# Issuing one third of the FFN weight reloads from GpSimd instead of SyncE in a macaron block

## The reference

```python
x = x + 0.5 * ffn(layernorm(x))
x = x + attn(layernorm(x))
x = x + 0.5 * ffn(layernorm(x))      # the same weights as the first

def ffn(x):                          # 2048 tokens a core
    shared = sum over 2 experts of (silu(x @ wg_s) * (x @ wu_s)) @ wd_s    # 512 wide
    probs  = softmax(x @ router_w);  comb = the top 2 of 16, normalised
    routed = sum over 16 experts of comb[e] * (silu(x @ wg_r[e]) * (x @ wu_r[e])) @ wd_r[e]   # 256 wide
    return shared + routed           # every routed expert is computed for every token
```

## Time and profile before

| | us |
|---|---|
| median of 3 runs | 4065.6 |
| the runs | 3907.1, 4065.6, 4118.3 |
| the profiled execution, its own time | 3765.1 |
| its span, slowest core (core 3) | 3763.6 |
| spans of the 8 cores | 3729.9 to 3763.6 |

### The profile page before, as it was taken

One profiled execution on the slowest core, in us unless ns is written; L12 is line 12 of the kernel. 1 busy time (PEld: TensorE's weight loads), 2 busy tenths in 40 slices (PEclk: granted clock), 3 DMA queues, 4 the chain that ended last, 5 costly groups with the idle time before them and its releaser, 6 DMA issues. The chain is left out here.

```text
span 3763.6 us, 36251 instructions; the slowest of 8 cores (3729.9 to 3763.6 us)
## 1 busy us (share of the span) xinstructions
PE 2747.7 (73%) x12680; PEld 1178.4 (31%) x12680; DVE 1110.7 (30%) x2412; ACT 1016.2 (27%) x1035; POOL 172.9 (5%) x265
## 2 busy tenths in 40 slices
PE   0235676999999736776776676756626999999996
PEld 0112222444444312222222222213312444444443
DVE  2331100303223204445344444442323213031220
ACT  2300000101011045566566556551131101010110
POOL 0001110000000000110010010010000000000000
PEclk9567888999999958887888887889957999999998
DMA  3069987645455323323323322232105456464655
GB/s 114 2 92 164 172 171 173 186 135 185 145 168 173 95 30 59 55 61 59 56 60 59 62 54 56 49 51 22 12 0 141 156 158 183 162 160 144 174 156 179
DMA packets 207457, 407.87 MB, mean 108 GB/s; under 512 B 59904, under 2 KB 109312, under 8 KB 207120
## 3 DMA queue, kind: packets, MB, share of 16 engines
q1 hardware_dynamic: 96080, 316.24, 28.4%
q0 software_dynamic: 101968, 52.61, 12.5%
q10 hardware_dynamic: 9232, 36.70, 3.6%
HBM read 405.00 MB, written 40.37 MB: 118 GB/s over the span
## 5 line engine op out<-in xcount | busy, mean ns | idle before, releaser
L548 PE MATMUL f_p<-hf,f_wgu 128*128 128x512 bf16 x2560 | 605.2, 391 | 128.7 <-DMA f_wgu<-wu_r 92.5
L625 PE MATMUL f_p<-f_pall,f_wdb 128*128 128x512 bf16 x2560 | 574.4, 388 | 54.4 <-DMA f_wdb<-wd_r 32.4
L559 PE MATMUL f_p<-hf,f_wgu 128*128 128x512 bf16 x2560 | 578.6, 379 | 0.0
L1085 ACT ACTIVATE at_pexp<-at_ps,at_ngm 128x1024 bf16<-128x1024 f32 x512 | 532.6, 1114 | 104.6 <-PE at_ps L1054 87.4
L1105 DVE TENSOR_TENSOR at_pt<-at_pexp,at_e 128x512 bf16<-128x512 bf16 x1024 | 387.8, 422 | 307.3 <-ACT at_pexp L1085 275.4
L579 ACT ACTIVATE f_gs<-f_p 128x1024 bf16<-128x1024 f32 x160 | 164.0, 1025 | 1066.6 <-PE f_p L548 1066.6
L548 PEld LDWEIGHTS f_p<-hf,f_wgu 128*128 128x128 bf16 x2560 | 255.3, 100 | 453.8 <-issue 172.4
L1034 PE MATMUL at_ppr<-at_pt,at_vtm 128*65 128x512 bf16 x1024 | 346.3, 456 | 69.8 <-DVE at_pt L1105 69.8
L625 PEld LDWEIGHTS f_p<-f_pall,f_wdb 128*128 128x128 bf16 x2560 | 253.5, 100 | 375.3 <-issue 88.9
L587 DVE TENSOR_TENSOR f_t<-f_p,f_bc 128x1024 f32<-128x1024 f32 x128 | 156.8, 1225 | 706.4 <-PE f_p L559 706.4
L559 PEld LDWEIGHTS f_p<-hf,f_wgu 128*128 128x128 bf16 x2560 | 250.4, 98 | 302.1
(11 more groups left out here) (106 smaller groups left out, 1387.5 us busy)
## 6 DMA issues: line engine op xcount, KB each, us to landing
f_wgu<-wbf_scr SPq DMA_DIRECT2D x140, 1024.0 KB, 6.1
f_wdb<-wbf_scr SPq DMA_DIRECT2D x140, 512.0 KB, 4.2
f_bc<-comb_scr SPq DMA_DIRECT2D x128, 256.0 KB, 6.5
wbf_scr<-f_wgu SPq DMA_DIRECT2D x20, 1024.0 KB, 8.0
at_e<-etab_scr SPq DMA_DIRECT2D x32, 608.0 KB, 4.3
at_e<-etab_scr ACTq DMA_DIRECT2D x32, 608.0 KB, 4.6
wbf_scr<-f_wdb SPq DMA_DIRECT2D x20, 512.0 KB, 5.6
xt<-x ACTq DMA_DIRECT2D x1, 8192.0 KB, 41.0
```

Of the source, the lines that this page charges most:

```text
L548: pg=pg, tb=tb: h.matmul(pg[:, mc * 512: mc * 512 + 512], wgu[buf][:, c * 256 + mc * 128: c * 256 + mc * 128 + 128], hf[:, c * S + tb * TB ...
L559: pu=pu, tb=tb: h.matmul(pu[:, mc * 512: mc * 512 + 512], wgu[buf][:, 2048 + c * 256 + mc * 128: 2048 + c * 256 + mc * 128 + 128], hf[:, c ...
L625: mc=mc, po=po, col=col, u=u: h.matmul(po[:, col: col + 512], wdb[buf][:, mc * 1024 + dch * 128: mc * 1024 + dch * 128 + 128], p_all[:, u ...
L1085: hh=h_: h.activation(out=pexp[:, (q % 2) * 2048 + half_i * 1024: (q % 2) * 2048 + half_i * 1024 + 1024], in_=p_s[:, half_i * 1024: half_i ...
```

## The change

A table gives each buffer the engine that issues its reloads: buffers 0 and 2 stay with SP, buffer 1 goes to POOL. That holds for `wgu` and `wdb`, in the 7 blocks that are not fresh. The waits of a load go with it to the engine that issues it. The `bc` loads stay on SP. In each block 7 of 20 units use buffer 1 (u = 1, 4, 7, 10, 13, 16, 19), so 49 loads of `wgu` and 49 of `wdb` move.

Second, in the first call the weight loads of units 0 to 2 of the fresh block are written ahead of the loop over the blocks by a call with `wonly`, and are skipped (`skipw`) when the loop comes to them. The dictionaries are defined further up; they issue nothing.

```diff
+                WQUEUE = ("sync", "gpsimd", "sync")
...
+                pre_issued = first_call
...
-                def issue_gu(tb, u):
+                def issue_gu(tb, u, wonly=False, skipw=False):
...
-                    if fresh:
+                    if skipw:
+                        pass
+                    elif fresh:
                         if gu_free[buf] is not None:
                             ph.wait("gpsimd", gu_free[buf])
...
                     else:
+                        qw = WQUEUE[buf]
                         if gu_free[buf] is not None:
-                            ph.wait("sync", gu_free[buf])
-                        ph.wait("sync", wb_ev[(u, 0)])
+                            ph.wait(qw, gu_free[buf])
+                        ph.wait(qw, wb_ev[(u, 0)])
                         gu_dma[(tb, u)] = [ph.dma(
-                            "sync", wgu[buf][:, :],
+                            qw, wgu[buf][:, :],
...
+                    if wonly:
+                        return
                     if u < NE:
...
                     else:
+                        qw = WQUEUE[buf]
                         if wd_free[buf] is not None:
-                            ph.wait("sync", wd_free[buf])
-                        ph.wait("sync", wb_ev[(u, 2)])
+                            ph.wait(qw, wd_free[buf])
+                        ph.wait(qw, wb_ev[(u, 2)])
                         wd_dma[(tb, u)] = [ph.dma(
-                            "sync", wdb[buf][:, :],
+                            qw, wdb[buf][:, :],
...
+                if first_call:
+                    for u0 in range(3):
+                        issue_gu(0, u0, wonly=True)
...
-                    issue_gu(tb, 0)
-                    issue_gu(tb, 1)
-                    issue_gu(tb, 2)
+                    issue_gu(tb, 0, skipw=pre_issued)
+                    issue_gu(tb, 1, skipw=pre_issued)
+                    issue_gu(tb, 2, skipw=pre_issued)
+                    pre_issued = False
```

More of the change, by code:

```diff
@@ L385, in ffn_phase @@
                        for i in range(3)]
+                gu_dma, wd_dma, bc_dma = {}, {}, {}
+                gu_free = [None, None, None]
+                wd_free = [None, None, None]
+                bc_free = [None, None, None]
+                pre_issued = first_call
                 ev_prev = None
```

## The result

The changed kernel takes 1.0096 times the time of before, 95% interval 1.0058 to 1.0133: about 36 us more, and clear of no change, though less than 2%. The median of 14 runs is 3827.5 us, beside 3793.8 over 15 runs of before. The three runs of before that stand ahead of the prediction were among the high ones of the 15, the profiled execution (3765.1) among the low ones.

The account below looks back on a forecast made before the run. TensorE was taken as the bound. Terms 0 + 0 + 0 + 3.5 - 0.8 = +2.7 us on 3765.1 gave 3767.8, ratio 1.0007; applied to the median 4065.6, 4068 us, range 3915 to 4135.

Parts of the forecast that it names:

- Parts 1 to 3: Fresh block's early loads, 49 wgu reloads and 49 wdb reloads from POOL: each taken to cost 0 us.
- The fresh rows: POOL's loads in the fresh block, used as upper bounds: up half 24.2 us, wdb median 6.9, worst 11.0.
- The port lock: VectorE's two-port instructions, by a skill rule, delay GpSimd's descriptor writes and so its transfers; nothing was added for it.
- Part 4: Block borders: unit 19's POOL load runs beside SP's earlier next-block loads; 0.5 us in 7 blocks, +3.5 us.
- Its own sign of being right: Down pass: any TensorE idle time on wdb reloads is at unit 19 and adds to less than 10 us.
- unit 19 behind SP's early loads: Rival at block borders: POOL's load is served after SP's 2.75 MB; 5.8 us each, 41 us in all; chance 0.05.
- The slack: Block borders: unit 19's load, issued by POOL at 844.8, has 6.9 us until its matmuls start at 851.7.
- The even share: Block borders: SP's and POOL's queues each get half of 224 GB/s, so unit 19's load lands in 6.5 us.
- The rate: Block borders: the DMA engines together move 224 GB/s while the next block's loads run.
- Part 5: Second FFN's start: wgu0 lands sooner without wgu1 beside it; 0 to 0.8 us gained, 0.8 taken, outer bound 7.9.

Follow-up runs that it names:

- e8: The kernel before with only the early fresh-block wgu loads written as in the changed kernel, all reloads on SP; ratio 1.0021 (0.9974 to 1.0068).
- e10: Changed kernel; SP's next-block loads held until unit 16 is done, POOL's wgu1 until unit 19's load lands; no undisturbed run, 38 waits, middle 2.5 us.
- e3: Changed kernel, but SP holds the next block's loads until unit 16 is done, issuing together with POOL; one undisturbed run, 3792.8 us.
- e9: The kernel before, with the second call's first three wgu loads issued from SP ahead of its router wait; too few runs for a ratio, lowest 3770.1 us.
- e2: Changed kernel, but SP issues nothing for the next block until unit 19's wdb load has landed; two undisturbed runs, 3789.0 and 3804.9 us, no ratio.
- e6: Changed kernel, but SP issues only 1.25 MB of the next block's loads before unit 19's load has landed; one undisturbed run, 3801.6 us.
- e5: Changed kernel, but buffer 1's wdb loads are issued from ACT's queue instead of POOL's; one undisturbed run, 3833.8 us.

## Why the prediction was wrong

**Parts 1 to 3 held.** For the early loads no effect is shown (e8). `wgu` from POOL lands in 6.0 us, under the slack of 13.8, and TensorE never waits for it inside the blocks; `wdb` from POOL lands in 4.1 us (middle), better than the 5.9 that was taken and far from the fresh rows' 6.9. The fresh rows were bounds of another kind of transfer, and leaving their far end without weight was right. The port lock did not show either: L607, the product that was L595, takes 1225 ns beside POOL's issues. No run shows that this product is in a two-port mode at all, so it rules out a cost here and doesn't test the rule. The row of the page (core 1):

```profile
L607 DVE TENSOR_TENSOR f_pall<-f_t,f_gs 128x1024 bf16<-128x1024 f32 x128 | 156.8, 1225 | 11.8
```

**Part 4 is the step that failed** in the account of the change, in the size of its term: 0.5 us in each of 7 blocks, +3.5 us, where 34.0 were measured on core 7. Its own sign of being right, less than 10 us of idle time at unit 19, was passed with 23.5. Its place was right to the transfer, and the rival "unit 19 behind SP's early loads" named the mechanism and came to 41 us, 29 in five borders. These went into the miss:
- The number of borders is five. The last block of a call has no next one.
- The slack. Unit 19's matmuls were put at 851.7, two units after POOL's issue; by the earlier trace rows unit 19 ends at 854.71, so they start at about 851.1. The slack is 6.4 us and not 6.9.
- The landing. The even share between two queues gave 6.5 us (its upper end, with the 5.3 of the earlier trace rows, adds to 8.1, not 7.9); 8.7 to 12.2 were measured on cores 4 to 7, middle 9.8, and 8.7 in e10, where the two queues had nothing else of this core beside them. The rival's sum, 9.0 for what is ahead plus 3.7, gave 12.7.
- The rate. 224 GB/s was taken from the earlier trace rows, a mean over 22 us with idle engines in it; 290 to 316 GB/s were moved while the loads ran. This one went the other way and is why the rival was too high: by an estimate at 300 GB/s, some 1.05 MB are through when POOL issues, and the other 1.7 MB and 3.7 us make 9.4 us.
- The clock. Behind the waits of core 7 the same 16 matmuls take 4.9 to 6.4 us instead of 3.6. That was left out of every term, and is 10.5 of the 34.0 us.

The rule of the Trainium skill (DMA: Bandwidth & Descriptors, section SWDGE vs HWDGE vs iDMA), by which an engine goes round between the queues, was used to choose the even share over the rival. That the turns give equal shares of bytes was the prediction's own step, and that step is what e3 and e10 refute: the landings there have middles of 8.9 and 8.7 us, not 6.5. The chance of 0.05 for the rival rested on a rule and not on a row, as the text itself said.

**Part 5** took 0.8 us of gain, and none is seen: the wait is 6.3 to 8.4 us in the changed kernel and 6.2 to 7.9 before, over the eight cores. The neighbour that was taken away was not what made it long; the place behind the router was, as e9 shows.

**The range** failed by another step, and a larger one: the base. The forecast of 4068 us, range 3915 to 4135, stood on 4065.6, the median of three runs; over 15 runs the median of before is 3793.8, 272 us lower, and 3827.5 was measured after. Part 4's error is some 30 us and has the other sign, so with the right term the range would have missed as well. All three runs were among the high ones of the 15. The profiled execution was set aside, though it was the evidence that runs of 3765 us exist. That the change stays within 2% came out right, at a price that Part 4 didn't have.

## What to carry to other kernels

When loads are split over two queues, write out for each border between loops what is issued ahead of the last transfer that is still needed; a single queue had kept that order for nothing. A load with little slack must not be issued behind large ones that aren't urgent; a queue of its own, GpSimd's or ACT's, did not help it here. Hold the prefetch of the next stage until it has landed, or leave both in one queue in the order of need. And price a wait of TensorE with the slower matmuls behind it, not only with its own length.

## What the runs showed of the hardware

- A 512 KB load issued at nearly the same moment as 2.75 MB on another queue lands 6.2 to 14.5 us later, middle 8.7 (e10), against 3.8 to 5.3, middle 4.2, with only 1 MB behind it in its own queue (e2).
- How the engines divide their time is left open, but three simple rules are excluded: equal shares of bytes for the two queues (6.5 us, e10); shares in proportion to what each queue has outstanding (in e10 `wgu2` lands 2.8 to 8.2 us after the small load, 40 of 40); and a strict order of issue (in the changed kernel `wgu2` is issued 1.2 to 2.1 us ahead of unit 19's load, and on cores 4 to 7 it lands after it in 19 of 20).
- The queue of ACT behaves in this like that of GpSimd (middle wait 4.5 and 4.1 us).
- Cores differ at the same border: in e6 core 7 waits for 16.2 us in all and core 5 for none. What they share outside the core was not tested.
- What a wait costs in TensorE's clock is not set by its length alone. In the changed kernel the 16 matmuls take 3.61 us behind a wait of 3.05 and 5.30 behind one of 3.09 (core 6), and 6.54 behind one of 3.02 (core 5); in e5, core 4, a wait of 2.00 us is followed by 5.30, with the granted clock at 1.00 ahead of it and at 0.52, the level of 1.2 GHz, from 1080 to 1082. On core 7 of the changed kernel the waits of 3.51 to 5.94 us are followed by 4.92 to 6.37.
